# Adaptive-norm block with sparse attention: value products moved into the maximum search

## The reference

```python
q = _split_heads(x @ Wq + bq)
k = _split_heads(x @ Wk + bk)
v = _split_heads(x @ Wv + bv)
scores = jnp.einsum('bhqd,bhkd->bhqk', q, k) * scale
sparsity = scores.max(axis=-1) - scores.mean(axis=-1)
_, top_idx = jax.lax.top_k(sparsity, U)          # U = 307 of 2048 queries, per head
q_sel = jnp.take_along_axis(q, top_idx[..., None], axis=2)
attn = jax.nn.softmax(jnp.einsum('bhud,bhkd->bhuk', q_sel, k) * scale, axis=-1)
out_sel = jnp.einsum('bhuk,bhkd->bhud', attn, v)
out = jnp.zeros_like(q).at[bi, hi, top_idx].set(out_sel)
```

## Time and profile before

| | us |
|---|---|
| median of three runs | 1721.07 (1720.02 to 1728.72) |
| the profiled execution | 1707.33 |
| its span in the trace | 1705.2 |
| PE busy | 1511.2 (89%) |
| DVE busy | 1243.7 (73%) |
| ACT busy | 1031.6 (60%) |
| POOL busy | 302.4 (18%) |

### The profile page before, as it was taken

How to read it: one execution, slowest core, us unless ns; L and a number is a source line. 1 busy time by engine, 2 the same in 40 slices (tenths; PEclk the granted TensorE clock), 3 DMA queues, 4 the chain that set the end, 5 groups by cost and what they waited for, 6 DMA issues and landing times.

```text
span 1705.2 us, 28768 instructions
## 1 busy us (share of the span) xinstructions
PE 1511.2 (89%) x8650; PEld 846.4 (50%) x8650; DVE 1243.7 (73%) x2937; ACT 1031.6 (60%) x1380; POOL 302.4 (18%) x363
## 2 busy tenths in 40 slices
PE   2779999998859998999999769999899999989999
PEld 1342222222435542222222545543588987469988
DVE  3659999999767858999999777876755452665511
ACT  2338888887736667888888426773333374334364
POOL 1370000000733445000000223442111100011100
PEclk7889999999979999999999879999999999999999
DMA  9441111112331120111112201111034302004410
GB/s 239 178 130 34 41 37 49 44 37 74 121 101 47 52 72 26 48 45 37 41 50 76 62 26 46 52 40 62 13 102 158 126 32 80 0 25 157 157 47 31
DMA packets 91789, 119.25 MB, mean 70 GB/s; under 512 B 21346, under 2 KB 77378, under 8 KB 91204
## 3 DMA queue, kind: packets, MB, share of 16 engines
q1 hardware_dynamic: 88644, 117.73, 22.9%
q0 software_dynamic: 3072, 0.66, 0.4%
HBM read 93.54 MB, written 24.78 MB: 69 GB/s over the span
## 4 chain that ended last, share of the span: by engine, by line
PE 42%; DVE 32%; issue 13%; DMA 5%; ACT 4%; SPq 2%; POOL 1%; PEld 0%; DVEq 0%; ACTq 0%; PEldq 0%; POOLq 0%
DVE work_area L1080 23%; PE psum L1884 6%; PE psum L1822 6%; PE psum L1666 4%; PE psum L1689 4%; PE psum L1765 4%; PE psum L1678 3%; PE psum L1833 3%; PE psum L1842 3%; DVE big_area L1080 2%; PE psum L1525 2%; DMA work_area<-heads_out 2%; PE psum L1874 2%; DVE work_area L1161 1%; ACT big_area L800 1%
## 5 line engine op out<-in xcount | busy, mean ns | idle before, releaser
L1080 DVE CUSTOM_DVE_ANT_0 work_area<-psum,work_area 128x1024 f32<-128x1024 f32 x512 | 589.6, 1220 | 18.4 <-PE psum L1572 14.6
L734 ACT ACTIVATE work_area<-psum 128x1024 f32<-128x1024 f32 x512 | 510.9, 1027 | 88.8 <-DVE big_area L1080 33.1
L1572 PE MATMUL psum<-work_area 96*128 96x512 bf16 x1024 | 312.0, 387 | 47.9 <-DVE big_area L1080 7.6
L1562 PE MATMUL psum<-work_area 96*128 96x512 bf16 x1024 | 309.7, 385 | 12.8 <-DMA work_area<-q_parts 6.8
L752 ACT ACTIVATE work_area<-psum 128x614 f32<-128x614 f32 x256 | 164.1, 681 | 79.4 <-PE psum L1678 78.8
L1572 PEld LDWEIGHTS psum<-work_area 96*128 96x128 bf16 x1024 | 64.4, 98 | 267.3 <-DVE big_area L1080 249.2
L1562 PEld LDWEIGHTS psum<-work_area 96*128 96x128 bf16 x1024 | 89.9, 98 | 161.0 <-ACT work_area L734 57.6
L609 POOL DMA_INDIRECT heads_out<-work_area x96 | 99.1, 1032 | 145.7 <-DVE work_area L1244 124.4
L1215 DVE TENSOR_SCALAR big_area<-iota,rank 128x308 bf16<-128x308 f16 x512 | 122.0, 312 | 0.0
L1822 PE MATMUL psum<-work_area,xn 128*128 128x128 f32 x1024 | 117.3, 275 | 0.0
L1765 PE MATMUL psum<-slots_T,work_area 128*128 128x512 f32 x256 | 116.6, 599 | 0.0
(11 more groups left out here) (236 smaller groups left out, 1994.4 us busy)
## 6 DMA issues: line engine op xcount, KB each, us to landing
work_area<-in_L_ffn_w_dram SPq DMA_DIRECT2D x32, 1024.0 KB, 5.4
work_area<-q_parts SPq DMA_DIRECT2D x192, 64.0 KB
k_parts<-work_area SPq DMA_DIRECT2D x24, 384.0 KB, 3.2
work_area<-k_parts SPq DMA_DIRECT2D x32, 192.8 KB
q_parts<-work_area SPq DMA_DIRECT2D x16, 384.0 KB, 2.5
big_area<-q_parts SPq DMA_DIRECT2D x16, 384.0 KB, 7.3
work_area<-k_parts SPq DMA_DIRECT2D x32, 192.0 KB
work_area<-k_parts SPq DMA_DIRECT2D x32, 128.5 KB
```

What stands on the lines that cost most here:

```text
L734: s.activation(SC[:, t % 4], PS[:, 2 * (n % 2):2 * (n % 2) + 2].rearrange("p a n -> p (a n)"), ACT.Relu).then_inc(relu_done, 1)
L1080: v.tensor_tensor_reduce(SC[:, t % 4], PS[:, 4 + 2 * (t % 2):6 + 2 * (t % 2)].rearrange("p a n -> p (a n)"), SC[:, t % 4], 1.0, -3.0e38, A ...
L1562: last = mm(PS[:, 2 * (n % 2) + k], QS1[par][0:TERMS, t * P:(t + 1) * P], KS[par][0:TERMS, k * 512:(k + 1) * 512], start=True, stop=True)
L1572: last = mm(PS[:, 4 + 2 * (t % 2) + k], QS1[par][0:TERMS, t * P:(t + 1) * P], KS[par][0:TERMS, K1 + k * 512:K1 + (k + 1) * 512], start=Tru ...
```

## The change

The value products of both batches leave their places and go into the pseudo tile: head h of a batch's search forms value tile h, into the second bank of the pair whose first bank takes the means. ScalarE copies the value tile ahead of the means. The wait of `value_tile` on earlier copies goes, as the pair's own waits cover it. The search's loops over heads are written out on TensorE and ScalarE. The keys of a head are loaded in six copies of 16 rows instead of three of 48, 32 and 16. On POOL the biases of batch 0 come after the first two normalisations of batch 1, and those of batch 1 ahead of the shifts.

```diff
                 for n in (3, 2, 1):
-                    sp.dma_start(KS[par][at:at + n * DH, 0:K1 + HALF], k_parts[b][0:n, bass.ds(h0, DH), 0:K1 + HALF]).then_inc(kq_in[par], 16)
-                    at += n * DH
+                    for r in range(n):
+                        sp.dma_start(KS[par][at:at + DH, 0:K1 + HALF], k_parts[b][r, bass.ds(h0, DH), 0:K1 + HALF]).then_inc(kq_in[par], 16)
+                        at += DH
...
-            for t in range(NT):
-                value_bias(0, t)
             pool.wait_ge(ln1_ready, 2)
             for k in range(2):
                 normalised(1, k)
+            for t in range(NT):
+                value_bias(0, t)
             shifts(0)
...
-            shifts(1)
             for t in range(NT):
                 value_bias(1, t)
+            shifts(1)
...
-                s.activation(V[:, token_tile(t), :, 0:DH], PS[:, t % 2, 0:D].rearrange("p (h d) -> p h d", h=H), ACT.Identity).then_inc(v_copied, 1)
+                s.activation(V[:, token_tile(t), :, 0:DH], PS[:, 2 * (t % 2) + 1, 0:D].rearrange("p (h d) -> p h d", h=H), ACT.Identity).then_inc(v_copied, 1)
...
+                for h in range(H):
+                    for t in range(NT + 1):
+                        n = h * (NT + 1) + t
+                        act.wait_ge(diff_ready, b * (H * 17) + n + 1)
+                        if t < NT:
+
+                            act.wait_ge(max_done, b * (H * NT) + h * NT + t + 1)
+                            s.activation(SC[:, t % 4], PS[:, 2 * (n % 2):2 * (n % 2) + 2].rearrange("p a n -> p (a n)"), ACT.Relu).then_inc(relu_done, 1)
+                        else:
+                            take_values(b, h)
+                            s.activation(SMN[:, h], PS[:, 2 * (n % 2), 0:NT], ACT.Identity).then_inc(relu_done, 1)
...
             for u in range(NU):
                 first_part(0, u)
-            for t in range(NT):
-                take_values(0, t)
             deviations(1)
             maxima(0)
...
                 take_natural(1, q)
-                take_values(1, q)
                 take_heads(0, q)
...
             def value_tile(b, t):
-                if t > 1:
-                    pe.wait_ge(v_copied, b * NT + t - 1)
                 for cc in range(DC):
-                    last = mm(PS[:, t % 2, 0:D], hT_tile(t // G, cc, t % G), Wvs[:, cc], start=(cc == 0), stop=(cc == DC - 1))
+                    last = mm(PS[:, 2 * (t % 2) + 1, 0:D], hT_tile(t // G, cc, t % G), Wvs[:, cc], start=(cc == 0), stop=(cc == DC - 1))
...
                     else:
+                        value_tile(b, i * 2 + par0)
                         for tt in range(NT):
...
-                with pe.Fori(0, PAIRS - 1) as i:
-                    for par in range(2):
-                        pe_maxima(i, par, False)
-                pe_maxima(PAIRS - 1, 0, False)
-                pe_maxima(PAIRS - 1, 1, True)
+                for h in range(H):
+                    pe_maxima(h // 2, h % 2, h == H - 1)
...
-                        value_tile(1, q)
                         turn_heads(0, q)
...
             pe.wait_ge(kbarp_ready, 1)
-            for t in range(NT):
-                value_tile(0, t)
             pe.wait_ge(resid_ready, NU)
-            pe.wait_ge(v_copied, NT)
             maxima(0)
```

More of the change, by code:

```diff
@@ L724, in maxima @@
             def maxima(b):
-                with act.Fori(0, PAIRS) as i:
-                    n = 0
-                    for par in range(2):
[L729 to L737, removed]
+                for h in range(H):
[8 more added lines that the diff above has]
+                            s.activation(SMN[:, h], PS[:, 2 * (n % 2), 0:NT], ACT.Identity).then_inc(relu_done, 1)
             def attend(b):
@@ L1555, in differences @@
                     n = par * (NT + 1) + t
+                    par0 = par
                     par %= 2
                     if t == 0:
-                        pe.wait_ge(kq_in[par], b * (PAIRS * 144) + i * 144 + (144 if n < 34 else 288))
+                        pe.wait_ge(kq_in[par], b * (PAIRS * 192) + i * 192 + (192 if n < 34 else 384))
                     pe.wait_ge(relu_done, b * (H * 17) + i * 34 + (n + 1))
```

## The result

The changed kernel took 1732.62 us, median of 20 runs (1727.85 to 1737.23), against 1724.12 us of 20 runs of the kernel before beside them (1718.68 to 1730.22). The ratio is 1.0045, with a 95% interval of 1.0032 to 1.0058: 7.8 us slower, 5.5 to 10.0. That is a real loss, and it lies just inside the 0.5% (8.6 us) that the prediction took as the least that can be told from no change.

What follows compares the result with a forecast made beforehand. VectorE's row maximum was taken to bound both searches. Value products +18.3, key transfers -5.2, second selection -1.8 and written-out search -0.6 sum to +10.7 us on the median of 1721.07: 1731.8 us, range 1720 to 1743.

Steps and rivals of the forecast that it cites:

- Value products, +18.3: At each head's end in both searches, products in the pseudo tile delay VectorE by 0.58 us: +18.3 us for both batches.
- Search written out, -0.6: At the search's loop back edges, 7 a batch, writing out the heads saves -0.6 us in all.
- rival four: At each head's end, 0.21 us goes with ScalarE's loop while value products cost nearly nothing: 1713.6 us, chance 0.08.
- Rival three: In the search, written-out code stalls its fetch on TensorE, a third of a microsecond a head: +11, 1743 us, chance 0.09.
- Key transfers, -5.2: At the first search's start, six even key copies land sooner, first product at 117.1 instead of 122.3: -5.2 us.
- Alone it brings nothing: Ahead of the first search, removing 14 us of TensorE's value products gains nothing, since TensorE waited for data until 122.31.
- Second selection, -1.8: In the second batch's selection, removing value products shortens VectorE's waits by 1.2 and 0.62: -1.8 us, between -0.6 and -3.
- The sum: Over the whole kernel, 18.3 - 5.2 - 1.8 - 0.6 = +10.7 us, giving 1731.8 us.
- Rival one: Ahead of tile 14's first half, the value product costs nearly nothing, 0.2 us a head: 1720 us, chance 0.16.
- two: At the first search's start, memory holds the landing back, so no earlier start: +16.6, 1737.7 us, chance 0.15.
- Slower by over 0.5%: For the whole kernel, a loss above what a measurement can tell from no change, 8.6 us: chance 0.55.

Runs made afterwards that it cites:

- Experiments 4: The changed kernel with the second batch's value products back in its selection: ratio 1.0016 to the kernel before, +2.8 us.
- 6: The changed kernel with every value product in the pseudo tile formed twice: ratio 1.0204 to the kernel before, +35.2 us.
- 9: The changed kernel with each head's value product moved behind tile 14's first half: 1742.19 us, ratio 1.0113 to the kernel before.
- experiment 3: The kernel before with only the search written out on TensorE and ScalarE: ratio 0.9981, -3.3 us.
- experiment 2: The changed kernel with the old key copies of 48, 32 and 16 rows: ratio 1.0079 to the kernel before, +13.6 us.
- Experiment 1: The kernel before with only the six even key copies, value products in their old places: ratio 0.997, -5.2 us.
- experiment 5: The kernel before with even key copies and the search written out, value products in their old places: 1714.9 us, ratio 0.994.
- experiment 7: The kernel before with even key copies, search written out and the attention's key copies made even too: 1714.55 us, ratio 0.994.
- experiment 8: The kernel before profiled once more, unchanged: 1722.68 us, span 1720.6.

## Why the prediction came out as it did

The direction and the mechanism were right; the time of 1731.8 us lies 0.8 from the median of 1732.62. That closeness is in part luck, since the kernel before had 1724.12 in the runs beside it and not 1721.07: the sum was +10.7, measured are +7.8.

- **Value products, +18.3.** Right. Predicted 0.58 us a head, measured 0.56 against the kernel that is written out otherwise (18.99 - 18.43), or 2 x (15 x 0.56 + 0.37) = 17.5. Tile 14 was 0.37 late (forecast 0.43). The slack ahead of the mean is 0.87 - 0.55 = 0.32 where the wait of 0.25 in the earlier trace rows was taken: the next head's difference starts 1.14 us behind tile 13, 0.55 later than the 0.59 of the earlier trace rows. Experiments 4, 6 and 9 tell the same. ScalarE's copy and POOL's bias were hidden as said.
- **Search written out, -0.6.** This is the step that was mis-sized: -3.2, by experiment 3. The working took the earlier trace rows for code that is written out, but only TensorE's was; the text of rival four said so and gave that way 0.08. Of the 0.21 us lost at a head's end about 0.1 went with ScalarE's loop. Rival three's stall did not come: written out, every head takes 18.43 or 18.44 us but a search's first, at a low clock, and one or two later ones (18.61 and 18.63), which are as much longer in the loop; and the looped heads are 0.01 to 0.05 us longer where the edge is. The Trainium skill, "Runtime: NRT & Kernel Launch", section "Instruction fetch mechanics", has a taken branch stall on a fetch; no row here shows such a stall.
- **Key transfers, -5.2.** Right: 5.9 us by the first product (122.31 to 116.39), of which 5.6 by the time from issue to product, and 5.8 by the results of experiment 2 and the change. The step's forecast of 7.9 us from issue to product was 7.49. Experiment 1's 5.2 is no second proof of the number, as by rows 2.4 us of its gain come from the clock. What the prediction left out is the clock: once the data arrive early, the removed products would have kept TensorE at its full clock into the search (experiment 5). "Alone it brings nothing" was right against the kernel before, which started at 0.50 too, but it gives away 1.9 us that even keys alone win (experiments 1 and 5).
- **Second selection, -1.8.** About -1.3, well within the bounds. The wait of 1.55 us that it was read from was itself only 1.11 in the next profile of the same code, and the steadiest gain was at a place that the prediction did not look at: VectorE's wait for the sum in the second round, 1.05 or 1.06 in all seven profiles with value products in the stage, 0.28 in all four without. The wait of 1.55 comes out at 0.90 to 1.66 in the seven, at 0.98 in the four.
- **The sum.** -5.9 + 17.5 - 3.2 - 1.3 = +7.1, in the measured 5.5 to 10.0. Rival one (nothing for the products), two (no earlier start), three and four are out, but for the half of four that lies in ScalarE's loop. Slower by over 0.5% was given 0.55, and the result, 0.45%, is not that: the 2.6 us of the mis-sized step make the difference.

Keys even and search written out, without moving the products, gives 1714.9 us (experiment 5), the fastest of these kernels together with experiment 7.

## What to carry to other kernels

Idle time of an engine inside a bound stage is worth what is free at the one place where work is put: TensorE had 28 us to spare in a search, 14 us of products were put there, and 8.8 of them came out again as time. Follow the chain from the insertion point to the bounding engine's next start, with durations from that very spot, before moving work into slack; and when a stage's start is moved forward by faster loads, look again at what used to keep an engine at its full clock ahead of it.

## What the runs showed of the hardware that was not expected

- **TensorE's first products after idling.** With 15.4 us of idleness ahead, the granted clock was 0.50 and stood at it for the first 4.24 us; with 1.2 us it was 1.00, and the same products led to the first maximum 1.27 us sooner. The first head lost a further 0.59. In the kernel before 6.78 us of idleness had the same effect, 0.50 for the 4.33 us up to the first maximum.
- **Written-out code in place of a loop on ScalarE** brought the next head's first Relu from 0.71 to 0.63 us behind its difference, at every head. Whether the constant in the wait or the missing loop does it was not separated.
- **The attention has two paces in the same code.** The first batch's attention takes 7.96 us a head in the first profile of before and 9.1 in all ten others, from the third to the fifth head on. The second batch's differs too: mostly 7.95 to 8.1 us a head in the first profile of before, 8.3 to 8.5 with single heads of 9.1 in most others, 9.05 in experiment 7. In the slower one ScalarE's exponential (L752) starts late behind its scores (L1671). The changed kernel's timeline:

```profile
574.30 0.69 PE L1671 MATMUL psum<-work_area 99*128 99x307 bf16 x4
...
576.37 1.89 ACT L752 ACTIVATE work_area<-psum 128x614 f32<-128x614 f32 x3 [2.45 <-PE psum L1671]
```

and the same place in the kernel before:

```profile
569.74 0.69 PE L1678 MATMUL psum<-work_area 99*128 99x307 bf16 x4
570.20 1.26 ACT L752 ACTIVATE work_area<-psum 128x614 f32<-128x614 f32 x2 [0.85 <-PE psum L1678]
```

2.07 us instead of 0.46 between the starts, once a head. It is not the code (experiment 8), nor the spread of the keys' loads (7), nor TensorE's clock, which is 1.00 from 520 to 640 us in both profiles of before; the cause stays open. It makes 11 or 12 heads x 1.15 = 13 to 14 us, about as much as the runs of one kernel differ, so a single profile of this kernel can't carry a comparison of totals.
